# Paired context projections in three cross attentions, and another form of the routing, in a one-core decoder

## The reference

```python
q = (x @ Wq).reshape(B, Sq, h, d).transpose(0, 2, 1, 3)
k = (context @ Wk).reshape(B, -1, h, d).transpose(0, 2, 1, 3)
v = (context @ Wv).reshape(B, -1, h, d).transpose(0, 2, 1, 3)
scores = jnp.einsum('bhid,bhjd->bhij', q, k) * scale
attn = jax.nn.softmax(scores, axis=-1)
out = jnp.einsum('bhij,bhjd->bhid', attn, v)
out = out.transpose(0, 2, 1, 3).reshape(B, Sq, h * d)
return out @ Wo + bo
```

```python
logits = xf @ Wr + br
topk_val, topk_idx = jax.lax.top_k(logits, K)
scores = jax.nn.softmax(topk_val, axis=-1)
...
out = jnp.sum(gathered * scores[:, :, None], axis=1)
```

## Time and profile before

| | us |
|---|---|
| median of 3 runs (lowest to highest) | 3226.33 (3225.44 to 3230.64) |
| the profiled execution | 3226.89 |
| its span in the trace | 3224.9 |

### The profile page before, as it was taken

How to read it: one execution, slowest core, us unless ns; L and a number is a source line. 1 busy time by engine, 2 the same in 40 slices (tenths; PEclk the granted TensorE clock), 3 DMA queues, 4 the chain that set the end, 5 groups by cost and what they waited for, 6 DMA issues and landing times. The chain is left out here.

```text
span 3224.9 us, 56903 instructions
## 1 busy us (share of the span) xinstructions
PE 2751.6 (85%) x18629; PEld 2001.9 (62%) x18630; DVE 1469.0 (46%) x3482; ACT 1287.2 (40%) x3853; POOL 892.0 (28%) x574
## 2 busy tenths in 40 slices
PE   5656999979787989999589877899959997989899
PEld 2345666656455655555489744566648996776566
DVE  5686888831634233333422276666641003663211
ACT  1324777722432123333223222677733332772211
POOL 3254555510001022222123244455422222330000
PEclk8867999969798999999789987999968998999899
DMA  2000000000240010000247701000044555003000
GB/s 100 1 1 26 16 13 12 8 28 0 71 104 30 0 42 11 14 11 7 105 164 240 224 35 31 21 19 14 15 163 139 179 180 144 1 28 97 28 26 23
DMA packets 107206, 191.23 MB, mean 59 GB/s; under 512 B 56020, under 2 KB 80804, under 8 KB 95316
## 3 DMA queue, kind: packets, MB, share of 16 engines
q1 hardware_dynamic: 92834, 163.68, 16.0%
q0 software_dynamic: 6816, 18.62, 1.9%
q10 hardware_dynamic: 7442, 7.47, 0.8%
HBM read 171.04 MB, written 18.71 MB: 59 GB/s over the span
## 5 line engine op out<-in xcount | busy, mean ns | idle before, releaser
L1363 POOL TENSOR_TENSOR L_xattn_p<-L_xattn_p,L_xattn_ri 112x1500 f32<-112x1500 f32 (+1 forms) x192 | 435.8, 2270 | 645.5 <-DVE L_xattn_ri L1621 645.5
L1519 ACT ACTIVATE L_xattn_pT<-ps 125x448 f32<-125x448 f32 (+1 forms) x576 | 254.9, 476 | 373.5 <-PE ps L1437 373.4
L1531 ACT ACTIVATE L_xattn_p<-L_xattn_sa,L_xattn_ng 112x375 f32<-112x375 f32 x512 | 304.9, 598 | 70.4 <-DVE L_xattn_ng L1650 51.6
L1437 PEld LDWEIGHTS ps<-ident,L_xattn_p 112*125 112x125 f32 x1920 | 254.2, 190 | 115.5 <-ACT L_xattn_pT L1519 34.9
L1437 PE MATMUL ps<-ident,L_xattn_p 112*125 112x112 f32 x1920 | 296.1, 285 | 21.0 <-ACT L_xattn_pT L1519 11.0
L1004 PEld LDWEIGHTS ps<-L_ffn_xsT,L_ffn_w 128*128 128x128 f32 x2240 | 265.2, 195 | 7.0 <-issue 1.9
L1004 PE MATMUL ps<-L_ffn_xsT,L_ffn_w 128*128 128x128 f32 x2240 | 266.2, 278 | 2.4 <-ACT L_ffn_xsT L1034 2.4
L273 POOL TENSOR_TENSOR ln_rstd<-ln_tmp,half 112x8 f32<-112x8 f32 x26 | 44.4, 1720 | 716.0 <-DVE ln_tmp L222 537.1
L1066 DVE TENSOR_TENSOR L_ffn_y<-ps,L_ffn_pack 128x256 f32<-128x256 f32 x70 | 29.7, 425 | 365.1 <-PE ps L1013 365.1
L1013 PE MATMUL ps<-L_ffn_weights,L_ffn_hT 128*128 x840 | 192.9, 379 | 2.3 <-DVE L_ffn_hT L1078 2.3
L1457 PE MATMUL ps<-L_xattn_kT,L_xattn_qm 32*112 32x375 f32 (+1 forms) x1280 | 173.1, 523 | 4.2 <-DVE L_xattn_ng L1647 1.9
(11 more groups left out here) (407 smaller groups left out, 5265.1 us busy)
## 6 DMA issues: line engine op xcount, KB each, us to landing
L_ffn_w<-in_L_ffn_experts SPq DMA_DIRECT2D x74, 1024.0 KB, 5.2
L_attn_toeplitz<-L_attn_h SPq DMA_DIRECT2D x4, 3136.0 KB, 24.4
L_xattn_src<-in_ctx SPq DMA_DIRECT2D x32, 281.2 KB, 2.9
L_ffn_weights<-in_L_ffn_experts SPq DMA_DIRECT2D x8, 1028.0 KB, 16.5
L_xattn_src<-in_ctx SPq DMA_DIRECT2D x16, 375.0 KB, 3.0
L_xattn_keys<-in_ctx SPq DMA_DIRECT2D x16, 281.2 KB, 5.8
L_xattn_rows<-in_ctx_rows SPq DMA_DIRECT2D x16, 281.2 KB
L_ffn_weights<-in_L_ffn_experts SPq DMA_DIRECT2D x8, 516.0 KB, 9.3
```

What stands on the lines that cost most here:

```text
L1363: g.tensor_tensor(P[:, m % 4, :, :], P[:, m % 4, :, :], ri[:, m % 4, :].unsqueeze(2).broadcast_to([T, W, S2]), ALU.mult).then_inc(s["prob_ ...
L1437: last = pe.transpose(turned(t)[:, j * T:(j + 1) * T], P[:, m % 4, j, kc * KW:(kc + 1) * KW], k.ident[0:T, 0:T])
L1519: act.activation(PT[:, m % 4, kc, :, :].rearrange("p h t -> p (h t)"), turned(t), ACT.Copy).then_inc(s["pt_ev_a"].sem, 1)
L1531: last = act.activation(P[:, n % 4, j, :], at, ACT.Exp, bias=ng[:, n % 4, j:j + 1], scale=-1.0 if mask else 1.0, accum_out=rs[:, n % 4, j: ...
```

## The change

**Cross attentions.** All three take the paired form: context rows are loaded as 128 and the doubled rest. The bias row in the context (a POOL memset) is gone; DVE adds bv where there is one. Jobs are ordered anew: for W = 4, V0 (tiles 0 and 1 of V as a pair) of the running batch at step 0, the K pair of the next batch at step 1, V2 and the next Q at step 2, O at step 3; for W = 2, V0 at step 0, V2 and Q at step 1, K's first pair at step 2, second pair and O at step 3. Pairs use banks 6 and 7 for W = 4; for W = 2 they use the two banks of the scores of the unit before (`job_bank`). Values are weighed every second unit everywhere (`PVS`). With `LATE` (layers 0 and 2) exponentials lag one unit, transposes three and weighing five. O gets signals of its own, `wo_mm` and `res_done`.

```diff
-        places = {(0, "a"): ("K", 0), (0, "b"): ("V", 2), (1, "a"): ("O", 0), (1, "b"): ("Q", 0), (3, "b"): ("V", 0)}
-    elif W == 4:
-        places = {(0, "a"): ("K", 0), (0, "b"): ("K", 1), (1, "a"): ("O", 0), (1, "b"): ("Q", 0),
-                  (2, "b"): ("V", 0), (3, "a"): ("V", 1), (3, "b"): ("V", 2)}
+    if W == 4:
+        jobs = [("V", 0, 0, 0), ("K", 0, 1, 1), ("V", 2, 0, 2), ("Q", 0, 1, 2)]
...
+        jobs = [("V", 0, 0, 0), ("V", 2, 0, 1), ("Q", 0, 1, 1), ("K", 0, 1, 2), ("K", 2, 1, 3)]
+    ONE, TWO = 6, 7
+    TURN, OUT, PVS = 2 + LATE, 3 + 2 * LATE, 2
...
+    def job_bank(n):
+
+        return ONE if W == 4 else 2 * ((n - 1) % 2)
+
```

The two halves of a pair, and what they wait for:

```diff
+            def rest_rows(kind, c, u, bank):
+
+                for h, (to, cols, t) in enumerate(parts(kind, c, bank)):
+                    rows = slice(64 * h, 64 * h + 64)
+                    if kind == "K":
+                        pe.matmul(k.ps[:, to, cols], wk[rows, 1, t * KP:(t + 1) * KP], src[rows, u, 1, :], start=True,
+                                  stop=False)
+                    else:
+                        pe.matmul(k.ps[0:KW, to, cols], src[rows, u, 1, t * KW:(t + 1) * KW], wv[rows, 1, cols],
+                                  start=True, stop=False)
+
...
+            def open_pair(i, n):
+                what = job_at(i, n, "KV")
                 if what is None:
                     return
                 kind, c, b, u, count = what
-                pe.wait_ge(*job_out.at(count - 1))
-                if paired and (kind, c) == order[J_V]:
-                    project(kind, c, b, u, 6)
+                if W == 4:
+                    pe.wait_ge(*job_out.at(count - 1))
+                    if (kind, c) == ("V", 0):
+                        pe.wait_ge(*s["res_done"].at(b - 2))
+                        pe.wait_ge(*s["ot_ev"].at(b - 1))
+                else:
+                    pe.wait_ge(*s["exp_done"].at(i * U + n))
+                context_there(kind, c, b + 1, u)
+                rest_rows(kind, c, u, job_bank(n))
+
...
+                else:
+                    pe.wait_ge(*s["exp_done"].at(i * U + n - 1))
+                    pair = job_at(i, n - 1, "KV") if not (isinstance(b, int) and n == 0 and b == 0) else None
+                    if pair is not None:
+                        pe.wait_ge(*job_out.at(pair[4]))
+                c, e, strips = heads(p)
+                for j in strips:
```

The order within a step on PE, and on ACT and DVE the lag:

```diff
+                b, u, p = batch_of(i, n)
+                early = W == 2 or p == jobs[J_V2][3]
+                score(i, n)
                 if W == 2:
-                    job(i, n, "a", first, last_turn)
...
-                    turn_over(i, n - TURN, (0, 1), first)
-                    job(i, n, "b", first, last_turn)
-                    turn_over(i, n - TURN, (2,), first)
+                    open_pair(i, n)
+                weigh(i, n - OUT, first, b)
+                if W == 4 and early:
+                    open_pair(i, n)
+                    close_pair(i, n)
+                turn_over(i, n - TURN, (0, 1), first)
+                if W == 4 and not early:
+                    open_pair(i, n)
+                if W == 2 or not early:
+                    close_pair(i, n)
+                ask(i, n)
+                answer(i, n, first)
+                turn_over(i, n - TURN, (2,), first)
...
                 store_turned(i, n - TURN, (0, 1), first)
-                exponentials(i, n, (0,))
+                exponentials(i, n - LATE, (0,), first)
                 store_turned(i, n - TURN, (2,), first)
-                exponentials(i, n, range(1, HALVES))
+                exponentials(i, n - LATE, range(1, HALVES), first)
```

```diff
                     with pe.Fori(0, B // 4) as i:
                         for u in range(4):
                             turn(4 * i + u, u)
+                if router_w is not None:
+                    pe.wait_ge(*k["pack_in"].at(32))
+                    pe.wait_ge(*nev.at(B))
+                    for c in range(2):
+                        for g in range(G):
+                            last = pe.matmul(k.ps[g * LANE:(g + 1) * LANE, 6, 0:GT], router_w[:, c, :],
+                                             k.XT[:, c, g * GT:(g + 1) * GT], start=(c == 0), stop=(c == 1))
+                    last.then_inc(k["gb_mm"].sem, 1)
+                    pe.wait_ge(*k["gs_copied"].at(1))
+                    for j in range(GB):
+                        last = pe.transpose(k.ps[0:T, 7, j * KP:(j + 1) * KP], logits[:, j * T:(j + 1) * T],
+                                            k.ident[:, :])
 
             @block.scalar
             def _(act):
```

```diff
                     other = lg[:, :, e:e + 1]
                     if e + 1 < E:
-                        v.tensor_tensor(cmp[:, :, e + 1:E], other.broadcast_to([T, B, E - e - 1]),
+                        v.tensor_tensor(cmp[:, :, e + 1:E, e], other.broadcast_to([T, B, E - e - 1]),
                                         lg[:, :, e + 1:E], ALU.is_ge)
-                    ch.link(v.tensor_tensor(cmp[:, :, 0:e + 1], other.broadcast_to([T, B, e + 1]),
-                                            lg[:, :, 0:e + 1], ALU.is_gt))
-                    ch.link(v.tensor_tensor(ahead[:, :, :], ahead[:, :, :], cmp[:, :, :], ALU.add))
+                    last = v.tensor_tensor(cmp[:, :, 0:e + 1, e], other.broadcast_to([T, B, e + 1]),
+                                           lg[:, :, 0:e + 1], ALU.is_gt)
+                ch.link(last)
+                ch.link(v.tensor_reduce(ahead[:, :, :], cmp[:, :, :, :], AX.X, ALU.add))
                 ch.link(v.tensor_scalar(ahead[:, :, :], ahead[:, :, :], 2.0, None, ALU.is_lt))
```

```diff
-                        last = pe.matmul(k.ps[0:KT, 6, 0:2 * (most - 1)], place[:, n, :],
-                                         owned[:, n, :, :].rearrange("p w q -> p (w q)"), start=(n == 0),
-                                         stop=(n == picks - 1))
+                        strip = slice(n % 2 * KT // 2, (n % 2 + 1) * KT // 2)
+                        last = pe.matmul(k.ps[strip, 6, 0:KT], owned[:, n, :], place[:, n, :], start=(n < 2),
+                                         stop=(n >= picks - 2))
                 last.then_inc(s["rg_listed"].sem, 1)
+                pe.wait_ge(*s["gs_copied"].at(1))
...
-                ch.link(last)
+                ch.link(v.tensor_scalar(base[:, :], chosen, 0.5 - KT / 2, 1.0 / KT, ALU.add, ALU.mult))
+                ch.link(v.tensor_scalar(base[:, :], base[:, :], WHOLE, None, ALU.add))
+                ch.link(v.tensor_scalar(base[:, :], base[:, :], WHOLE, float(KT), ALU.subtract, ALU.mult))
+                ch.link(v.tensor_tensor(rest[:, :], chosen, base[:, :], ALU.subtract))
                 for c in range(4):
...
+                    mine = owned[:, at, 0:tiles]
+                    ch.link(v.tensor_tensor(mine, along(base[:, at], tiles),
+                                            marks.unsqueeze(1).broadcast_to([T, part, tiles]), ALU.is_equal))
+                    v.tensor_tensor(mine, mine, along(ids[:, at], tiles), ALU.mult)
...
-                v.tensor_tensor(route.rows[:, 1, :], listed[:, 1, :], spare[:, :], ALU.add)
-                v.tensor_copy(route.rows[:, 0, :], listed[:, 0, :]).then_inc(s["rg_rows"].sem, 1)
+                v.wait_ge(*s["gt_tr"].at(1))
+                ch.link(v.tensor_copy(spare[:, :], k.ps[:, 7, 0:tiles]))
+                ch.link(v.tensor_tensor(row[:, :], k.ps[:, 7, KT // 2:KT // 2 + tiles], spare[:, :], ALU.add))
+                ch.link(v.tensor_scalar(far[:, :], row[:, :], N + 0.5, -float(N), ALU.is_gt, ALU.mult))
+                v.tensor_tensor(route.rows[:, 0, :], row[:, :], far[:, :], ALU.add).then_inc(s["rg_rows"].sem, 1)
```

578 lines of the change are left out of this document (275 added, 303 removed).

## The result

The changed kernel takes 3103.31 us (median of 4 runs, 3097.88 to 3105.24), against 3227.82 for the kernel before in the runs beside it: a ratio of 0.9611 with a 95% interval of 0.9595 to 0.9628. The forecast was 3122, with a range of 3090 to 3168. 124.5 us were gained where 104 were expected, so the time lies inside the range, near its low end.

What follows compares the result with a forecast made beforehand. PE was taken to bound the three context attentions, and a chain over DVE, PE and POOL the routing. 3226.9 - 59 (attentions) - 45 (routing) = 3122.8, the median 0.6 lower: 3122 us, range 3090 to 3168.

Steps and rivals of the forecast that it cites:

- PE's work in L1: L1 context attention: pairing K and V and weighing by two units takes 1.9 us a batch off PE's work.
- the pair's factor of 0.84: Context attentions: two 375-column K tiles cost 2.29 us paired against 2.74 unpaired; the factor was applied to V too.
- L1's waits: L1 context attention: scores wait for DVE's copies, 1.2 us after V0 and 0.9 after the first K pair.
- Rival (b): L1 context attention: DVE's copies hide after all, 22.8 us a batch, 25 us more gained, 3097; chance 0.10.
- L0's waits: L0 context attention: a later lag gives PE's waits about 5 us more slack; idle falls from 0.94 to 0.2.
- Rival (a): L0 and L2 attentions: waits only change place; L0 gains its work alone, 0.75 x 15, L2 nothing; 3160; chance 0.25.
- L2: L2 context attention: matmul work stays, idle falls from 1.84 to 0.15, period from 21.5 to 19.8 us a batch.
- Opening and closing: Ends of the attention stages: V leaves the opening and partly returns in the last batch; -1, -4 and -1 us.
- The logits' gain: Routed feed forwards: logits on four strips start the router earlier, -4.7 us in L0_ffn, -6.8 in L1_ffn, -6.5 in L2_ffn.
- Rival (c): Logits and slot tables: column strips don't run at once, +29 to +40 us, 3151 to 3163; chance 0.07.
- Router and slot tables: Routing: comparisons without waiting and one sum, -1.9 us in each of three routers; slot tables -10.4 in each of two stages.
- Rival (d): Context attentions: slower, as pair copies stand behind clamp and maxima on DVE; about 216 us lost, 3338; chance 0.04.

Runs made afterwards that it cites:

- ACT's edit: Changed kernel with ACT taking exponentials ahead of the copies of transposed parts in L0 and L2: 3054.55 us in one run.

## Why the prediction was right in its total and wrong in its parts

**PE's work in L1 was mis-sized.** I took the pair's factor of 0.84 from the earlier trace rows, where full rows and rest stood between groups of other kinds. In L1 a K pair costs 2.00 for 2.74, V 4.1 for 5.6, and four scores 0.72 for 0.82. Over a batch: scores -0.45, K -1.5, V -1.5, weighing -0.3, Q and O -0.2, transposes +0.1, together -3.8 instead of -1.9 (24.3 to 20.5 by the distances of the starts). The run with the rests moved gives 1.5 of it back by order alone, and at 24.22 lands at the 24.4 that I had forecast: the step that failed is the price of the pair, which I had read off with its neighbours' changes in it. The order accounts for 1.5 of the 1.9 that I had missed; the other 0.4 is not traced. I did see that change in the rows, 1.46 against 1.37, and priced it at 0.09, as a cost that grows; I did not ask where the new order makes fewer of them. The measured price is 0.19 for a change, half of it on each side: the 0.09 is one side. The Trainium skill (TensorEngine Tiling (Array Packing), Key Properties) says that changing the tiling mode drains TensorE; these runs agree that a change costs time, and put 0.19 us on it, but they don't show a drain as such.

**L1's waits were right**, in place, releaser and size. Rival (b), whose time fits L1 best (22.8), is wrong by its reason: the copies did not hide.

**L0's waits were wrong.** The step was "each of PE's waits for ACT or DVE gets about a unit, 5 us, more slack". Slack of a unit did not help on this ring through three engines' fixed orders: the idle time rose from 0.9 to 2.0 a batch instead of falling to 0.2. I had looked at each hand-over by itself, each bank with its copy, and not added up the closed path DVE, PE, ACT, DVE. Rival (a) came nearest, by its mechanism (waits change their place), and even it kept the work's gain of 0.75, of which 0.2 was left. K copy first and exponentials first each shorten that ring, and each shortens the period.

**L2 was right by two errors** that cancel: its work fell by 1.0, where I had none, and its idle time to 1.1 and not to 0.15. From start to start the transposes of a batch went from 6.84 to 6.16 us with the same count of 48 records, K, Q and O fell by 0.1 each, and V stayed at 2.7. The transposes stand beside other work than before; that this is the price of changes again, and of waits right behind a group, fits the runs but was not tested in L2. The idle time that is left stands ahead of the scores, for DVE's maxima, and the run with ACT's edit takes 0.8 of it. Whether the longer lag as such was needed was not tried: with the old one weighing would add up in bank 7 while a pair lies there.

**Opening and closing** went as said in kind; the periods times 15 make 3.3, 31 and 26.9 of the stages' 4.7, 33.0 and 22.5, so that the ends of the stages gave -1.4, -2 and +4.4 for -1, -4 and -1. Why L2's cost 4.4 more was not traced; L0 has the same extra lag and gained.

**The logits' gain** was underestimated by 2.6 us in L1_ffn and by 8.7 in the three stages, most of the 11 by which the routed stages beat the forecast: 16 records of four strips take 1.71 us where I had 3.3. They begin in fours, 0.38 us apart, so the four passes were right and the 0.8 for each was not: the granted clock was 1.00 there, and 0.50 at the row that my price comes from. The 32 transposes took 5.76 for an estimated 7.2. Strips do run at once: that is 0.107 us for a record of 448 columns, where one of 375 columns in a K pair's full rows takes 0.32 (1.28 / 4) at the same clock. Rival (c) is out for the logits, and for the slot tables by the starts in pairs. **Router and slot tables** came within 0.4 us each. The rest of L1_ffn's gain, about 1.4 us, lies behind the first gather and was not traced further. Rival (d) is out: no stage became slower.

**Slips in the working** that change nothing: by the earlier trace rows DVE's work in a batch of L0 is 17.4 us and not 17.3, and 3122 + 40 is 3162.

## What to carry to other kernels

When engines with fixed orders hand work round in a circle, follow each wait to what released it until the same instruction of the next batch is reached. If no engine stands idle within its own piece, that round holds the period, and an instruction that stands in it without need is the one to move. Here moving the exponentials on ACT ahead of its copies was worth 49 us in two stages, while moving transposes on PE cost 33. Matmuls placed between a producer and the reuse of its bank are cover; before moving them, name what else covers the copy. A price read from a trace contains its neighbours, so take it from start to start in the same surroundings, or count the changes of array layout apart.

## What the runs showed of the hardware

A change between groups of matmuls that use different rows of the array (64-row pairs, 112- to 128-row matmuls) cost 0.19 us, seen as 0.09 to 0.11 longer in the group on either side: 1.52 us for eight of them. Across such a change the next weights began to load together with their matmul (1311.32 for both); without one they began 0.09 us ahead of it. Four column strips of 32 took 0.107 us a record of 448 columns at full granted clock. Matmuls of 64 weight columns and 128 moving columns began 0.213 us apart at a granted clock of 0.50 and 0.109 at 1.00 on one column strip; on two strips they began in pairs, within 0.01 us of each other, and the pairs at these same distances. Matmuls of 128 weight columns and 72 moving columns, in the kernel before, began 0.213 us apart at 0.50 too.
